# Context stage and shared stage of a routed block in one program block, without the barrier between them

## The reference

```python
x = x + xattn(layernorm(x))   # "context": 4 groups of tokens by token id
x = x + ffn(layernorm(x))     # "shared" expert for all tokens, and 32 routed ones
# xattn, for the group e of a token, with C = ctx_2048[e] (512 x 512):
#   silu(h @ C.T) * (h @ C.T) @ C.T
# ffn: h = rmsnorm(hidden) * norm_w
#   scores = softmax(h @ gate_w.T); top 4 of 32 experts, weights made to sum to 1
#   routed = sum over the 4 of weight * (silu(g) * u) @ w2[e],  g, u = split(h @ w13[e])
#   shared = (silu(h @ sg) * (h @ su)) @ sd
#   out = hidden + routed + shared
```

## Time and profile before

| | us |
|---|---|
| Runs shown | 700.8, 700.16, 696.78 (median 700.16) |
| The profiled execution, its own time | 696.68 |
| Its span, first to last instruction | 694.8 |
| Busy in the span: PE, DVE, ACT, POOL | 632.7, 442.1, 366.8, 334.1 |
| Mean granted clock of TensorE | 0.978 of full |

### The profile page before, as it was taken

How to read it: one execution, slowest core, us unless ns; L and a number is a source line. 1 busy time by engine, 2 the same in 40 slices (tenths; PEclk the granted TensorE clock), 3 DMA queues, 4 the chain that set the end, 5 groups by cost and what they waited for, 6 DMA issues and landing times.

```text
span 694.8 us, 15275 instructions
## 1 busy us (share of the span) xinstructions
PE 632.7 (91%) x3242; PEld 512.0 (74%) x3243; DVE 442.1 (64%) x1023; ACT 366.8 (53%) x637; POOL 334.1 (48%) x373
## 2 busy tenths in 40 slices
PE   3589999994999999899999999999999999999990
PEld 2577877774877877688888887788788788787870
DVE  7658777673799998455575565765566565646530
ACT  4446656653534322456666556765566655647530
POOL 2735777753002111544635556546555546565632
PEclk9999999996999999999999999999999999999996
DMA  6511222243784653667899698997777998978545
GB/s 249 194 32 56 104 84 99 108 166 141 248 314 51 147 137 46 139 181 210 229 269 237 191 274 218 281 278 192 217 201 194 278 266 207 272 204 230 103 64 70
DMA packets 35790, 124.69 MB, mean 179 GB/s; under 512 B 4784, under 2 KB 5936, under 8 KB 31152
## 3 DMA queue, kind: packets, MB, share of 16 engines
q0 software_dynamic: 24256, 59.26, 38.7%
q1 hardware_dynamic: 11504, 65.09, 26.4%
HBM read 90.51 MB, written 39.06 MB: 186 GB/s over the span
## 4 chain that ended last, share of the span: by engine, by line
PE 41%; DMA 14%; issue 8%; DVE 4%; POOLq 2%; ACT 2%; POOL 1%; DVEq 1%; ACTq 1%
PE sps_gu L223 8%; PE sps_gu L225 8%; PE sps_gu L224 8%; DMA out<-r_oh,e_sidx 5%; DMA out<-normw,e_sidx 4%; PE sps_t L223 3%; PE sps_t L225 3%; PE sps_t L224 3%; DMA out<-r_rank,e_sidx 2%; PE sps_rank L921 2%; PE sps_table L921 1%; DMA both<-hb_dram,e_gidx 1%; PE sps_cols L921 1%; PE sps_table L976 1%; ACT wh L1117 1%
## 5 line engine op out<-in xcount | busy, mean ns | idle before, releaser
L1330 DVE TENSOR_TENSOR wl<-raw,wh x87 | 105.9, 1226 | 54.4 <-ACT wh L1117 47.7
L223 PE MATMUL sps_gu<-wh,s_xth 128*128 x320 | 132.6, 415 | 2.9 <-DVE s_xtl L1313 2.1
L225 PE MATMUL sps_gu<-wh,s_xtl 128*128 x320 | 125.9, 393 | 0.0
L224 PE MATMUL sps_gu<-wl,s_xth 128*128 x320 | 125.1, 391 | 0.0
L909 POOL DMA_INDIRECT out<-r_oh,e_sidx x40 | 68.0, 1700 | 91.5 <-issue 73.2
L1117 ACT ACTIVATE wh<-raw x87 | 91.4, 1061 | 15.2 <-issue 9.4
L895 POOL DMA_INDIRECT both<-hb_dram,e_gidx x76 | 82.4, 1085 | 31.4 <-issue 17.4
L1092 ACT ACTIVATE both<-sps_gu 128x256 f32<-128x256 f32 x80 | 30.7, 384 | 79.7 <-PE sps_gu L225 72.6
L223 PEld LDWEIGHTS sps_gu<-wh,s_xth 128*128 128x128 f32 x320 | 60.2, 188 | 14.7 <-issue 4.5
L225 PEld LDWEIGHTS sps_gu<-wh,s_xtl 128*128 128x128 f32 x320 | 60.0, 188 | 13.9
L223 PE MATMUL sps_t<-wh,s_ath 128*128 x160 | 69.6, 435 | 0.4
(11 more groups left out here) (317 smaller groups left out, 1439.3 us busy)
## 6 DMA issues: line engine op xcount, KB each, us to landing
raw<-in_experts_w SPq DMA_DIRECT2D x32, 1536.0 KB
craw<-in_ctx_w SPq DMA_DIRECT2D x4, 1024.0 KB, 7.6
both<-hb_dram SPq DMA_DIRECT2D x16, 256.0 KB, 4.0
out<-hb_dram SPq DMA_DIRECT2D x4, 1024.0 KB, 17.4
out<-both POOLq DMA_DIRECT2D x16, 256.0 KB, 3.9
both<-hb_dram,e_gidx POOLq DMA_INDIRECT x76
out<-r_oh,e_sidx POOLq DMA_INDIRECT x40
sraw<-in_sg SPq DMA_DIRECT2D x1, 512.0 KB
```

What stands on the lines that cost most here:

```text
L223: pe.matmul(acc, left_hi, right_hi, start=start, stop=False)
L224: pe.matmul(acc, left_hi, right_lo, start=False, stop=False)
L225: return pe.matmul(acc, left_lo, right_hi, start=False, stop=stop)
L1330: dve.tensor_tensor(m.wl[:, w, ROWS[part], :], m.raw[:, bass.ds(x % 2, 1), ROWS[part], :], m.wh[:, w, ROWS[part], :].bitcast(F32), ALU.sub ...
```

## The change

```diff
@@ build
         m.carry = lambda eng: eng.sem_inc(m.s["carried"], 1)
+        m.top = top
+        m.block = top.enter_context(nc.Block())
         with ExitStack() as st:
@@ context
-        s = semaphores(nc, st, "c_", (
+        s = m.c = semaphores(nc, m.top, "c_", (
@@
-        block = st.enter_context(nc.Block())
+        block = m.block
@@ context, PE
             pipeline(pe, pairs, [("t1", 3), ("g1", 4), ("t2", 5), ("g2", 6)], emit,
                      looked_up(pe, m.tab1[0:1, 0, :], BACK1, E1, expert))
-            pe.wait_ge(s["x2"], 2 * number_of_pairs(pe, m.tab1[0:1, 1, 0:1], MAX1))
-            keep_busy(pe, m, ps_z[0], WARM)
+            m.pe_tiles = 2 * pairs
@@ shared_routing_and_experts, PE
             for q in range(G // 2):
                 for i in (2 * q, 2 * q + 1):
+                    if i == 2:
+                        pe.wait_ge(m.c["x1"], m.pe_tiles)
                     pe.wait_ge(gx[i % RING], 16 * (i // RING + 1))
                     wait(pe, s["t1lo"], i - RING + 1)
                     turn(turned[i % RING], xg[:, i % RING], C).then_inc(s["t1"], 1)
```

## The result

Over 21 executions of each kernel the changed one took 694.42 us (median), the one before 698.11: a ratio of 0.995, 95% interval 0.9936 to 0.9964, 3.5 us faster. Two later comparisons of the same pair (12 executions of the changed kernel each) gave 0.9981 (0.9956 to 1.0006) and 0.9974 (0.9956 to 0.9992). The forecast was a gain of 1.2 us and a time of 697.4: right in sign, with the time inside the range. The gain was forecast too small, by a factor of three against the first comparison. Weighted by their intervals the three comparisons give a ratio of 0.9963, some 2.6 us (an estimate), twice the forecast. The profiled execution took 694.36 us.

A forecast was written before the change was run, and what follows sets the result against it. PE bounds the routing stage behind the boundary. Tile 8 at 170.9 (tile 4's rows) + 5.2 (two pairs) + 2.0 (cold clock) = 178.1 against 179.3 us gains 1.2: 698.6 - 1.2 = 697.4 us, range 693 to 702.

The forecast's parts named there:

- PE bound behind the boundary, tile 8 as the finish line: Routing stage: PE busy 18.80 of 19.00 us; work from tile 8's start is unchanged, so gain is read there.
- Tiles 0 to 3 off the path: Stage boundary on PE: 16 transposes done by 157.9 us behind the last product; some 3.4 us leaves the path.
- ACT late next, 3.33 us from the table load to the first logits: Boundary: table load from 163.23 us puts first logits at 166.6 us against 171.9, 5.3 us earlier.
- The jump about 0: Each engine's jump from context to shared part: bounds 0 and 3.2 us, taken as about 0, hidden by waits.
- The barrier cost 3.2 us: Stage boundary before: ACT and PE start within 0.04 us of each other, 3.2 us behind the last warm-up matmul.
- Rows of tile 4, 4.0 us from issue to use: SP's loads, released by scatter landing at 166.8 us: bounds 3.2 and 4.8, middle 4.0, tile 4 at 170.9.
- The clock, 2.0 us: PE from tile 4: full clock 4.6 us behind its start, losing 0.44 x 4.6 = 2.0 us.
- early clock: Rival, chance 0.14: PE warm soon after tile 4 thanks to the first logits; gain 2.5 to 3.5 us.
- Sum: Tile 8 starts at 170.9 + 5.2 + 2.0 = 178.1 us against 179.3: a gain of 1.2 us.
- Shifted code: Listed among the outcomes with chance 0.05; over 1% slower was put down to it.
- cold burst: Rival, chance 0.16: PE waits after first logits, clock climbs late, loss 3.6 us; 1.8 us slower, 700.4.
- Expert stage falls differently: Rival, chance 0.10: a start shifted by 1 us reorders weight loads against scatters, some us either way.

The follow-up runs named there:

- e1: Changed kernel, but PE keeps its wait for the last x2 and the 24 warm-up matmuls and turns tiles 0 to 3 behind them; ratio 0.9963.
- e5: Kernel before, with the context stage's block left without POOL's drain and the barrier kept; ratio 0.996.
- e12: Kernel before, both blocks left without POOL's drain, barriers and warm-up kept; 690.14 us against 696.86, ratio 0.9902.
- e10: Kernel before, without POOL's drain in the first block, the wait for the last x2 and the 24 warm-up matmuls; barrier kept; ratio 0.9967.
- e2: Kernel before, without the wait for the last x2 and the 24 warm-up matmuls; barrier and order kept; ratio 0.9996.
- e3: Changed kernel, with 140 small warm-up matmuls on PE between tile 3 and the first logits; ratio 0.9948.
- e11: The changed kernel unaltered, measured a third time; ratio 0.9974.
- e6: Changed kernel, with POOL's context order swapped: a tile's statistics (rstd2) ahead of the scatter of the tile two before; ratio 0.9967.
- e9: Changed kernel, with its one block left without POOL's drain at the end of the program; ratio 0.9944.
- e7: Changed kernel, with rows of tiles 4 to 7 loaded from input x without waiting for the scatters, so routing values differ; one execution, 698.37 us.
- e8: The changed kernel unaltered, measured once more with a second profile; ratio 0.9981.

## Why the prediction was right, and where not

- **PE bound behind the boundary, tile 8 as the finish line:** right. 3.64 us at tile 8; timed were 3.5, 1.3 and 1.8 us.
- **Tiles 0 to 3 off the path:** as forecast, done by 157.3 us; but e1 shows 0.1 us of worth, not 3.4 us of relieved path. PE's time was free.
- **ACT late next, 3.33 us from the table load to the first logits:** 165.68 - 162.32 = 3.36 us. Right, and the logits left PE 0.51 us of idle time before tile 4.
- **The jump about 0:** right where it can be seen: ACT's table load starts 0.02 us behind its last instruction, and SP issues tile 4's rows 0.05 us behind the landing of the last scatter (165.91 against 163.29 + 2.57).
- **The barrier cost 3.2 us:** the cause was wrong. Two engines starting together showed that a barrier released them, not what held it. It was POOL's drain, 4.32 us up to 168.3 us on line 260: without it the wait behind the warm-up is 0.41 us (e5, e12), and without the warm-up too the first transpose comes 4.36 us earlier (e10 against e2). The term entered the sum only as a bound of the jump, so this did not move the number.
- **Rows of tile 4, 4.0 us from issue to use:** measured 168.96 - 165.91 = 3.05 us. The lower bound (a load with gaps around it) was the right row; this term gives back 1.0 us.
- **The clock, 2.0 us:** mis-sized, and the larger miss. From tile 4 to tile 8 I forecast 7.2 us, the chain shows 174.76 - 168.96 = 5.8. The clock was full again near 169.0 us, as tile 4 began, so that it cost next to nothing; most of the 0.5 to 0.6 us above the 5.2 of before goes with tile 5's rows, whose transposes start 0.86 us behind tile 4's instead of directly behind them (e3, at full clock throughout, needs 6.0). The step that failed is counting the 4.6 us from tile 4's start: the first logits had started 3.4 us earlier. This is the rival "early clock", to which I gave 0.14, and the prediction's own sign of being wrong, a high clock before 172 us, came true. The cold case exists: full clock came 2.1 us behind tile 4 in e11 and 5.3 us in e6. With e3 no better than the changed kernel, its mean cost over executions is below what can be measured.
- **Sum:** 1.2 + 1.0 + 1.4 = 3.6 us at tile 8. The 4.6 us of cold clock are counted from tile 4's start, so the first logits earn nothing there. They did start at 0.50 (165.68 us), but 2.77 us of them were followed by full clock as tile 4 began in the profile of the changed kernel, and not in those of e6 and e11 (5.3 and 2.1 us behind tile 4). That they earn nothing is borne out in some executions only.
- **Shifted code, cold burst:** neither came. That code at other places would be fetched again in loops, to which I gave 0.05, was my guess; no run shows it. The pages of before and after count the same 12 and 18 packets on q8 and q14.
- **Expert stage falls differently:** it can't be ruled out. The 508.7 us from tile 8 to the last add, against 507.0, lie within the 505.8 to 512.1 of all profiles.

What stays open: why POOL's `DRAIN` takes 2.81 us at the end, with all adds landed, and 4.32 us at the boundary; whether e12 and e9 differ; and why the later comparisons timed less than the 3.2 to 3.7 us that the profiles of the changed kernel show at tile 8.

## What to carry to other kernels

When two engines with different last work start together, look for what holds the slowest at the barrier (here a `DRAIN` record of 4.32 us on POOL) before rewriting the order around it: here a flag in one place gave what the rewrite gave (0.996 against 0.995 to 0.998), and in two places 6.7 us. I would leave a drain out only where semaphores of your own already cover the data, as they do in e5, e9, e10 and e12; no run here tries it without them. Of a step moved into an engine's idle time count only what the next wait leaves over (e1: 0.1 us at tile 8). And an early load may sit beside the very transfer that frees your buffers (e7: its landing took 6.1 us instead of 3.7).

## What the runs showed of the hardware

- POOL's `DRAIN` on leaving the context stage's block took 4.32 us in before and in e2. The first transpose came 12.27 us behind x1 with it (e2) and 7.91 without (e10), 4.36 us. At the end of the program, with all adds landed, it took 2.81 us in the changed kernel (the span ends 8.5 to 9.0 us behind the start of the last add with it, 7.9 in e7 alone, and 5.8 and 6.0 without).
- Four 256 KB loads beside a 128-row scatter came with a landing of 6.1 us (e7), against 3.7 in the changed kernel; one profile of each.
- In these profiles the clock did not fall and rise at a fixed distance from what PE does. With the same boundary on PE it fell 1.5 us behind the last transpose in the changed kernel (158.8 against 157.3), 2.0 in e8, 3.4 in e11 and 4.4 in e9; before, it fell 3.6 us behind the last product. It rose 3.4 us behind the start of the first logits in the changed kernel, 3.9 in e8, 2.8 in e9 and 5.2 in e11.
- The 24 warm-up matmuls were followed by full clock sooner where PE went straight on. With the barrier held by the drain full clock came 10.6 us behind their start (before); where PE went on at once (0.41 us in e12 and e5, no gap in e1) it came 3.1 us behind it in e12 (164.0 against 160.92), 4.3 in e1 and 5.0 in e5. It gained nothing at tile 8 (19.55 in e5, 19.53 in e10 without them), since PE waited for rows.
